# Balanced experts: the second product with its weights stationary, bias at the eviction, result turned back, and the last experts in another order

## The reference, cut to what matters

```
norm   = layer_norm(feat)                       # 8192 x 128
scores = norm @ centroids.T                     # 8192 x 8
for e in range(8):                              # balanced: each expert takes 1024 tokens
    s = where(taken, -inf, scores[:, e])
    idx = top_k(s, 1024);  taken[idx] = True
routed = feat[idx of e]                         # 1024 x 128 for each expert
h = gelu(layer_norm(routed) @ w1[e] + b1[e])    # 1024 x 512
h = h @ w2[e] + b2[e]                           # 1024 x 128, the second product
out = routed + h                                # put back in token order
```

## Time and profile before

| | |
|---|---|
| runs of the kernel, median of 3 | 1427.29 us (1427.21 to 1427.66) |
| profiled execution: span from first to last instruction | 1485.4 us, 33918 instructions (its own time is given by the span alone) |
| busy in the profile | PE 78%, PEld 50%, DVE 61%, POOL 54%, ACT 47% |
| one turn of the second call, with seek and all pieces (turns 4, 6) | 29.53 and 30.73 us |
| last seek ends, second call | 1371.4 us |
| last scatter issued, second call | 1478.1 us |

### The profile page before, as it was taken

One profiled execution on the slowest core, in us unless ns is written; L12 is line 12 of the kernel. 1 busy time (PEld: TensorE's weight loads), 2 busy tenths in 40 slices (PEclk: granted clock), 3 DMA queues, 4 the chain that ended last, 5 costly groups with the idle time before them and its releaser, 6 DMA issues. The chain is left out here.

```text
span 1485.4 us, 33918 instructions
## 1 busy us (share of the span) xinstructions
PE 1157.9 (78%) x11356; PEld 745.3 (50%) x11356; DVE 901.1 (61%) x2806; ACT 701.1 (47%) x1485; POOL 809.1 (54%) x712
## 2 busy tenths in 40 slices
PE   0799999999999975468888680849996647888864
PEld 0244444444444433136676460739995315666743
DVE  4377767777777657787775004665556787777300
ACT  0467677676776745512223230945553722223222
POOL 0387878878788760036667751025551003667756
PEclk9999999999999997569999795869998757999977
DMA  6000000000000004403333325000000621333323
GB/s 166 8 2 0 0 0 0 0 0 0 0 0 0 1 2 129 131 20 51 50 52 66 58 25 120 0 0 1 0 0 21 173 71 26 51 66 53 56 46 28
DMA packets 82316, 54.64 MB, mean 37 GB/s; under 512 B 12865, under 2 KB 73665, under 8 KB 82241
## 3 DMA queue, kind: packets, MB, share of 16 engines
q1 hardware_dynamic: 59712, 36.89, 8.9%
q0 software_dynamic: 22528, 16.79, 8.7%
HBM read 28.49 MB, written 25.17 MB: 36 GB/s over the span
## 5 line engine op out<-in xcount | busy, mean ns | idle before, releaser
L352 POOL TENSOR_TENSOR patt_aa<-patt_aa,causal_aa 128x512 f32<-128x512 f32 x256 | 319.3, 1275 | 73.6 <-DVE patt_aa L476 71.8
L476 DVE TENSOR_TENSOR patt_aa<-p_second_aa,first_aa 128x512 f32<-128x512 f32 x384 | 247.3, 686 | 136.3 <-ACT first_aa L409 132.5
L409 ACT ACTIVATE first_aa<-p_first_aa 128x512 f32<-128x512 f32 x384 | 208.5, 596 | 139.0 <-PE p_first_aa L567 135.1
L1330 POOL DMA_INDIRECT rows_e<-norm_rows,index_e x128 | 127.3, 994 | 247.0 <-DVE index_e L1046 209.2
L567 PE MATMUL p_second_aa<-q_t_aa,k_t_aa 32*128 32x512 f32 x768 | 235.7, 642 | 0.0
L567 PE MATMUL p_first_aa<-q_t_aa,k_t_aa 32*128 32x512 f32 x768 | 217.4, 642 | 15.7 <-ACT first_aa L409 15.4
L1178 PE MATMUL p_y_e<-w_e,hid_e 128*128 128x128 f32 x1024 | 148.4, 287 | 12.7 <-issue 12.4
L586 PEld LDWEIGHTS p_z_aa<-patt_aa,v_aa 128*32 128x32 f32 x3072 | 72.4, 109 | 147.5 <-issue 80.4
L1246 PE MATMUL p_cnt_e<-reach_e,ones_e 128*128 128x240 bf16 x448 | 86.8, 324 | 75.8 <-DVE reach_e L1092 73.3
L1178 PEld LDWEIGHTS p_y_e<-w_e,hid_e 128*128 128x128 f32 x1024 | 134.1, 202 | 15.8 <-issue 15.7
L1168 PE MATMUL p_h_e<-rows_t_e,w_e 128*128 128x512 f32 x256 | 139.4, 662 | 0.1
(11 more groups left out here) (242 smaller groups left out, 2188.7 us busy)
## 6 DMA issues: line engine op xcount, KB each, us to landing
norm_rows<-norm_n SPq DMA_DIRECT2D x32, 256.0 KB, 2.4
w_e<-L_ffn_w SPq DMA_DIRECT2D x32, 256.0 KB
ffn_rows<-x SPq DMA_DIRECT2D x8, 512.0 KB, 3.2
x<-ffn_rows SPq DMA_DIRECT2D x8, 512.0 KB, 7.6
out<-x SPq DMA_DIRECT2D x8, 512.0 KB, 3.2
rows_e<-norm_rows,index_e POOLq DMA_INDIRECT x128
b_e<-L_ffn_b SPq DMA_DIRECT2D x16, 64.0 KB
ffn_rows<-yb_e,index_e POOLq DMA_INDIRECT x64
```

The lines of the kernel that those rows point to most:

```text
L352: pool.tensor_tensor(patt[n % LAG][:, b, :, :], patt[n % LAG][:, b, :, :], causal[:, None, :].broadcast_to([P, 4, P]), ALU.mult).then_inc( ...
L409: act.activation(first[n % 2][:, b, :], p_first[b][:], ACT.Identity).then_inc(first_copied, 1)
L476: dve.tensor_tensor(patt[n % LAG][:, b, :, :].rearrange("p h q -> p (h q)"), p_second[(2 * n + b) % ROOMS][:], first[n % 2][:, b, :], ALU. ...
L1330: pool.indirect_dma_start(rows[lpar][:, j, :], None, norm_rows, bass.IndirectOffsetOnAxis(ap=list_of(l, lpar)[:, j:j + 1], axis=0)).then_i ...
```

## The change

`down` is turned. Now w2 is stationary and 512 columns of the hidden tile stream, so `p_y[h]` holds y transposed (128 outputs x 512 tokens of half h) after four matmuls. ACT copies it with the bias as a per-partition operand to the new `y_t` (`copy_y_t`), PE turns it back with four transposes into the same PSUM room (`turn_y`), and ACT copies that to `yb` as before. `first_row`, its two memsets and the bias matmuls go; `b2` becomes one column. `plan` and `does` go; the turns are written out. The queue's loads wait for `y_t_copied` where they waited for `y_copied`.

```diff
-                    pe.matmul(p_y[t // 4][:, (t % 4) * D:(t % 4 + 1) * D], first_row[:], b2[par][:], start=True, stop=False)
-                    for f in range(FC):
-                        mm = pe.matmul(p_y[t // 4][:, (t % 4) * D:(t % 4 + 1) * D], hid[:, f, t * P:(t + 1) * P], w2[par][:, f, :],
-                                       start=False, stop=(f == FC - 1))
+                def down(c, h, fs):
+                    pe.wait_ge(gelu_done, 8 * c + 4 * h + 4)
+                    if c > 0 and fs[0] == 0:
+                        pe.wait_ge(y_copied, 2 * c - 1 + h)
+                    for f in fs:
+                        mm = pe.matmul(p_y[h][:], w2[c % 2][:, f, :], hid[:, f, h * 512:(h + 1) * 512],
+                                       start=(f == 0), stop=(f == FC - 1))
+                    if fs[-1] == FC - 1:
+                        mm.then_inc(down_done, 1)
+                def turn_y(c, h):
+                    pe.wait_ge(y_t_copied, 2 * c + h + 1)
+                    for j in range(4):
+                        mm = pe.transpose(p_y[h][:, j * P:(j + 1) * P], y_t[:, h, j * P:(j + 1) * P], k["ident"][:])
+                    mm.then_inc(y_turned, 1)
...
+                def copy_y_t(c, h):
+                    act.wait_ge(down_done, 2 * c + h + 1)
...
+                    act.activation(y_t[:, h, :], p_y[h][:], ACT.Identity, bias=b2[c % 2][:, 0:1]).then_inc(y_t_copied, 1)
...
+        def up_rooms(c):
+            return p_h if c < E - 3 else [*p_h, p_cnt]
```

More of the change, by code:

```diff
@@ L912, in experts, with list_of @@
         parts = 8
[L914 to L927, removed]
+        SEEKS = E - 1
+        def list_of(l):
             return index[l % 4]
-        SETUP = 11
+        def up_rooms(c):
+            return p_h if c < E - 3 else [*p_h, p_cnt]
+        SETUP = 9
         MARK_LINKS = 1 + 2 * PASSES + 2 * (HALF - 1) + 2 + 4 + 1
@@ L945, in store_x, with load @@
                         sp.dma_start(ffn_rows.rearrange("(n p) d -> p n d", p=P)[:, tiles, :], k["x"][:, tiles, :]).then_inc(x_stored, 16)
[L947 to L950, removed]
+                def load(e):
+                    par = e % 2
+                    at = slice(e, e + 1)
                     w1_src = d["L0_ffn_w1"][at, :, :].rearrange("a p f -> (a p) f")
@@ L961, in turn @@
                     sp.dma_start(b2[par][:], b2_src).then_inc(wl[par], 16)
-                    if e == 1:
-                        store_x()
-                plan(sp, turn)
+                load(0)
+                load(1)
+                store_x()
+                for e in range(2, E):
+                    load(e)
             @block.vector
@@ L1062, in note @@
                         ins.then_inc(sv, 1)
[L1064 to L1076, removed]
+                    at = slice(e, e + 1)
                     windows = [[] for _ in range(PASSES)]
-                    if lists:
-                        slots, parts, narrow, tiles_are, tiles, lane_chunk, copy_parts, result = listing(lists[0], 1 - par)
+                    if e > 0:
+                        slots, parts, narrow, tiles_are, tiles, lane_chunk, copy_parts, result = listing(e - 1, 1 - par)
                         chunks = [lambda c=c: lane_chunk(c) for c in range(CHUNKS // 2)]
@@ L1137, in turn @@
                     assert done[0] == SEARCH_LINKS, done
-                plan(dve, turn)
+                for e in range(SEEKS):
+                    seek(e)
+                dve.tensor_scalar(chosen[(E - 1) % 2][:], avail[:], 0.0, None, ALU.is_gt).then_inc(chosen_done, 1)
+                list_at_once(E - 2)
+                list_at_once(E - 1)
             @block.tensor
@@ new lines, in count @@
+                def count(e, n):
+                    for q in range(TILES // SPAN):
+                        if q % 2 == 0:
+                            pe.wait_ge(reached, 2 * PASSES * e + 2 * n + q // 2 + 1)
+                        mm = pe.matmul(p_cnt[:, 0:SPAN * CANDS], ones[:],
+                                       reach[:, q // 2, :, (q % 2) * SPAN:(q % 2 + 1) * SPAN],
+                                       start=(q == 0), stop=(q == TILES // SPAN - 1))
+                    mm.then_inc(counted, 1)
@@ L1252, in turn, with pieces @@
+                def pieces(e, n):
+                    if e > 0:
+                        listing_part(e - 1, n)
+                    if e > 2:
+                        late_part(e - 3, n)
+                    if e > 1:
+                        part(e - 2, n)
+                for e in range(SEEKS):
+                    for n in range(PASSES):
+                        count(e, n)
+                        pieces(e, n)
                         if n == HALF - 1:
@@ L1343, in turn @@
-                def turn(e, par, half):
-                    _, lists, compute = does(e)
-                    if compute and (not isinstance(e, int) or e > 2):
-                        for h in range(2):
-                            scatter(e - 3, 1 - par, half, h)
-                    if lists:
-                        gather(lists[0], 1 - par)
-                    for l in lists[1:]:
-                        gather(l, par)
-                    if isinstance(e, int) and e == E + 1:
-                        for h in range(2):
-                            scatter(e - 2, par, half, h)
@@ L1357, in _ @@
+                for e in range(1, SEEKS):
+                    if e > 2:
+                        scatter(e - 3)
+                    gather(e - 1)
+                gather(E - 2)
+                scatter(E - 4)
+                gather(E - 1)
+                scatter(E - 3)
+                scatter(E - 2)
+                scatter(E - 1)
                 for par in range(2):
```

348 lines of the change are left out of this document (195 added, 153 removed).

## The result

The changed kernel takes 1449.46 us (median of 4 runs, 1448.9 to 1451.12) where the kernel before takes 1427.42 beside it: ratio 1.0157, interval 1.0143 to 1.0172, **22 us slower**. The head of its page and two lines of its list of groups answer to the earlier trace rows: the wide product (L1165) and the transposes back (L1173) are busy 143 us in place of 202.5.

The account below looks back on a forecast made before the run. DVE was taken as the spine of the turns and POOL, not PE, as the bound of the tails. Median 1427.3 + 4 (seeks) + 10 (tail) = 1441 us; range 1410 to 1456, the forecast's own 1431 to 1456.

Parts of the forecast that it names:

- The 58 us are in no run: Expert layer's profile: the 58.1 us of span above the runs are recording delays, 54 of them from late PE news.
- The product itself: PE's `down`: 7.8 us instead of 8.9 per expert, a gain of 1.1, bound from 0 to 1.2.
- third per column: PE's matmuls: by the skill's issue gaps of 81 and 131 ns, wide ones would cost a third per column.
- lower bound of 0 for PE's gain: PE's `down`: the gain of 1.1 us per expert was bounded from 0 to 1.2.
- the prediction's own last rival: PE's `down` at 1.03 per wide matmul: 9.2 against 8.9, giving 1448 us; shares the forecast's chance of 0.58.
- The seeks, +4: Turns 3 to 6, both calls: +0.5 us per turn from shifted waits for counts, +4 in all, bounds -8 to +12.
- The tail, +10: After the last seek: POOL idles about 5 us per call for expert 6's index, +10 in all, bounds 0 to +14.
- hidden by the wait for the index: Tail: the gather of expert 5 ends 3 to 4 us later through later y, at no cost beside the index wait.
- Its sign of being right: Tail of the new profile: POOL idle some 2 us ahead of the gather of expert 6, then without waits.
- news late in every run, 1387: `down` during gathers: PE's late news is the chip's own, so the 54 us would go; 1387 us, chance 0.17.
- POOL quicker in the runs, 1417: Tails: POOL's transfers are shorter in runs than recorded, so PE ends them, 7 us less per call; chance 0.13.
- no change, 1429: Turns with a seek gain 1 us each instead of losing, -8 against the tail's +10; chance 0.12.

Follow-up runs that it names:

- narrow_down: The changed kernel with its turned product cut into matmuls of 128 columns, 32 narrow per expert instead of 8 wide; 1450.94 us, ratio 1.0171 to the kernel before.
- before_again: The kernel before, unchanged, recorded a second time; 1427.95 us, ratio 0.9999, span of the profile 1427.4.
- no_bias: The kernel before without the bias matmul of each tile, so b2 is not added; 1425.95 us, ratio 0.9992.
- pool_only: The kernel before with only POOL's order changed: gather of expert 6 ahead of the scatter of expert 4; 1430.16 us, ratio 1.0016.
- turn2_only: The changed kernel with expert 0's row turns and up products back at their old counts; 1446.75 us, ratio 1.0138 to the kernel before.
- old_pool: The changed kernel with POOL's old tail order: scatter of expert 4 ahead of the gather of expert 6; 1450.18 us, ratio 1.0162 to the kernel before.
- early_y: The changed kernel with the first half's transposes after count 2 instead of 3, ACT copying that half at once; 1439.13 us, ratio 1.0085 to the kernel before.
- late_last: The kernel before, but POOL's scatter of expert 3 waits for both halves of y instead of the first; 1441.58 us, ratio 1.0099.

## Why the prediction was right, and where it was not

Its direction and range hold; the value, 1441, is 8 us low.

- *The 58 us are in no run*: right, and the basis of the sign. That they come from recording narrow matmuls: wrong, by `narrow_down` and `before_again`. The undisturbed span of before shows what the prediction had to work out from rows with the late events taken off.
- *The product itself*: right. A pair of wide matmuls takes 1.72 from its start to that of the next count, and neither PE's load (`no_bias`) nor the width (`narrow_down`) moves the time by more than 2 us. Two slips stand beside it, and nothing rests on them: the "third per column" is two fifths by the two figures given there, and the lower bound of 0 for PE's gain leaves out the -0.3 of the prediction's own last rival.
- *The seeks, +4*: too small; turns 0 to 5 alone lengthen by 10.3 over both calls. At full clock a turn costs 0.6 to 0.94, not 0.5: tops +0.60 and count 1 -0.15, as forecast, and count 7 some +0.4, near it; but count 6, not priced, waits 0.16 more (half of the row turns now stands ahead of it), and count 0 gains 0.18 where 0.5 was booked (all from DVE's rows of turn 6). Turn 2, not counted at all, is 1.8 longer in the first call and 0.2 in the second, where this recording of before has 26.53 (25.43 in `pool_only`, whose turn 2 is the same); `turn2_only` gets 2.7 back. And among turns 3 to 5, one in each call has the lower clock in its middle (29.69 and 29.77), where the tops wait 2.8 to 2.9; the forecast had half clock only in its bounds. What makes the clock fall in these turns wasn't tried.
- *The tail, +10*: the size came out (+10.4 from the start of turn 6), the step did not, so the size is luck in part. The forecast had POOL wait for the index of expert 6 and called the later y "hidden by the wait for the index". It is the other way round: y of expert 3 is late, the gather of expert 5 starts 4.9 us later in its turn (second call), and by then the index is there. Its sign of being right, POOL idle some 2 us ahead of the gather of expert 6, didn't show. But the two waits end within 1.1 us of each other, so either would have given nearly this size, and 1.4 of the 10.4 is the lower clock in turn 6 of the first call. `old_pool` (no gain from the old order), `early_y` (the index wait appears once y is early) and `late_last` (late y alone costs 14.7) show it from three sides.
- *Rivals*: news late in every run, 1387, POOL quicker in the runs, 1417, and no change, 1429, fell with the sign. The one nearest in number, 1448 from a wide matmul at 1.03, has the wrong cause: they take 0.86. PE was through early, as forecast: ACT's last copy ends at 1421.1, 20.5 us ahead of POOL.

## What to carry to other kernels

Where an engine that works without slack ends the program, ask which result it waits for last before its final unbroken stretch, and put that result first: here making the first half of y come a pass earlier (`early_y`) gave 10 us, shorter turns included, while PE's cheaper product gave nothing that shows. A late item comes back through the loop it feeds (scatter, gather, rows, count), so delay cannot be booked as hidden until the engine behind it has been followed round. Of two waits that end close together only the later shows; removing it uncovers the other, as the index wait did.

## What was not expected of the hardware

Two recordings of one unchanged kernel have spans of 1485.4 and 1427.4 us, while its 31 runs beside the second lie between 1425.38 and 1429.04; the rows of the first hold waits that the second has not. A span far from the runs is a reason to record again before reading waits from it.
